# Two GNN and MoE layers on one core: the second layer's late expert tiles cut into four quarters in place of two halves

## The reference

```
x = x + gnn0(layernorm(x), adj, h0, y)
x = x + moe0(layernorm(x))        # 8 experts, hidden 512, top 2, plus a shared expert
x = x + gnn1(layernorm(x), adj, adj)
x = x + moe1(layernorm(x))        # 8 experts, hidden 256, top 2
```

```
h = gelu(xf @ w1[e] + b1[e]);  y = h @ w2[e] + b2[e];  out += cw[:, e] * y
```

## Time and profile before

| | |
|---|---|
| three timed runs, median (lowest, highest) | 1405.32 us (1403.5, 1409.83) |
| profiled execution, first to last instruction | 1406.8 us |
| PE busy | 1294.1 us, 92% |
| DVE busy | 922.4 us, 66% |
| ACT busy | 645.5 us, 46% |
| POOL busy | 426.3 us, 30% |
| scatters of y, both layers (L1882) | 144, 142.2 us, 987 ns each |
| granted clock of PE, mean | 0.977 |
| HBM read, written | 346.44 MB, 56.89 MB |

### The profile page before, as it was taken

One profiled execution on the slowest core, in us unless ns is written; L12 is line 12 of the kernel. 1 busy time (PEld: TensorE's weight loads), 2 busy tenths in 40 slices (PEclk: granted clock), 3 DMA queues, 4 the chain that ended last, 5 costly groups with the idle time before them and its releaser, 6 DMA issues.

```text
span 1406.8 us, 20911 instructions
## 1 busy us (share of the span) xinstructions
PE 1294.1 (92%) x6560; PEld 818.7 (58%) x6560; DVE 922.4 (66%) x2683; ACT 645.5 (46%) x1175; POOL 426.3 (30%) x427
## 2 busy tenths in 40 slices
PE   5899999999999999999989999999998999988950
PEld 2344445454545454554778998466666666766840
DVE  7776877777686877777542232877776777854323
ACT  3445444443434444343444554665555555543420
POOL 2102020202020202021365554302322333267772
PEclk9999999999999999999999999999999999999985
DMA  9798998889898979798559993789897988846846
GB/s 311 244 355 296 363 352 333 284 318 318 288 347 269 361 252 357 252 335 267 203 175 406 334 303 117 287 291 314 316 317 270 323 316 311 271 124 181 246 135 226
DMA packets 120974, 399.76 MB, mean 284 GB/s; under 512 B 19920, under 2 KB 51170, under 8 KB 91552
## 3 DMA queue, kind: packets, MB, share of 16 engines
q1 hardware_dynamic: 80512, 339.66, 69.1%
q10 hardware_dynamic: 28288, 34.98, 7.1%
q0 software_dynamic: 12064, 23.80, 4.6%
HBM read 346.44 MB, written 56.89 MB: 287 GB/s over the span
## 4 chain that ended last, share of the span: by engine, by line
PE 26%; DVE 11%; issue 8%; POOL 5%; DMA 2%; ACT 2%; POOLq 0%; SPq 0%; DVEq 0%; ACTq 0%
PE d L896 6%; POOL y_scratch L1882 3%; DVE adj_over_wb L398 3%; PE u L963 2%; PE agg L963 2%; PE u L880 2%; PE agg L968 1%; POOL rows_scratch L1873 1%; PE u L968 1%; PE agg L970 1%; PE agg L969 1%; PE u L970 1%; PE u L969 1%; PE u L882 1%; PE u L881 1%
## 5 line engine op out<-in xcount | busy, mean ns | idle before, releaser
L787 PE MATMUL agg<-m,xn 128*128 128x512 f32 (+1 forms) x800 | 402.8, 586 | 0.0
L1117 ACT ACTIVATE mabs<-m 128x512 f32<-128x512 f32 (+1 forms) x400 | 239.7, 617 | 309.4 <-DVE m L1635 208.6
L1635 DVE TENSOR_TENSOR m<-s,ring 128x512 f32<-128x512 f32 (+1 forms) x400 | 268.8, 675 | 149.0 <-PE s L763 128.1
L763 PE MATMUL s<-ymov,ysta 128*128 128x512 f32 (+1 forms) x400 | 263.3, 659 | 24.8 <-DVE m L1635 15.8
L1873 POOL DMA_INDIRECT rows_scratch<-xrow,idx x160 | 170.1, 1063 | 295.6 <-DVE xrow L1361 104.0
L787 PEld LDWEIGHTS agg<-m,xn 128*128 128x128 f32 x800 | 151.9, 190 | 68.5 <-issue 48.1
L1882 POOL DMA_INDIRECT y_scratch<-yo,ids x144 | 142.2, 987 | 83.5 <-issue 52.0
L763 PEld LDWEIGHTS s<-ymov,ysta 128*128 128x128 f32 x400 | 76.0, 190 | 153.7 <-issue 95.2
L398 DVE TENSOR_TENSOR adj_over_wb<-ring,adj_over_wb 128x512 fp32r<-128x512 f32 (+1 forms) x216 | 138.9, 673 | 34.5 <-ACT adj_over_wb L1220 32.1
L1220 ACT CAST adj_over_wb<-ring 128x512 fp32r<-128x512 f32 (+1 forms) x216 | 125.8, 607 | 52.4 <-PE agg L970 26.3
L1859 POOL TENSOR_TENSOR rstd<-vareps,mhalf 128x4 f32<-128x4 f32 x30 | 38.6, 1286 | 365.7 <-DVE vareps L1273 365.7
(11 more groups left out here) (278 smaller groups left out, 2270.3 us busy)
## 6 DMA issues: line engine op xcount, KB each, us to landing
ring<-in_adj_in SPq DMA_DIRECT2D x180, 1024.0 KB, 6.0
ring<-in_adj_out SPq DMA_DIRECT2D x30, 1024.0 KB, 7.8
rows_scratch<-yo ACTq DMA_DIRECT2D x81, 260.0 KB, 7.2
wb<-blob_scratch SPq DMA_DIRECT2D x24, 834.0 KB
stage<-in_adj_out SPq DMA_DIRECT2D x19, 1024.0 KB, 9.4
ring<-in_adj_in SPq DMA_DIRECT2D x20, 784.0 KB, 5.2
wb_more<-blob_scratch SPq DMA_DIRECT2D x15, 834.0 KB
xt<-rows_scratch SPq DMA_DIRECT2D x60, 130.0 KB, 4.1
```

Source lines behind the costliest of these rows:

```text
L763: pe.matmul(sbank[s % 2][:, 0:width(k)], ysta[:, s * P:(s + 1) * P], ymov[:, k % 2, 0:width(k)], start=True, stop=True).then_inc(s_made, 1)
L787: pe.matmul(abank[:, 0:n], xn[:, b, :], m[:, b % M_BUFS, 0:n], start=b == 0, stop=b == NB - 1).then_inc(S["agg_blocks"], 1)
L1117: act.activation(mabs[:, b % ABS_BUFS, 0:width(k)], m[:, b % M_BUFS, 0:width(k)], ACT.Abs).then_inc(abs_made, 1)
L1635: dve.tensor_tensor(m[:, s % M_BUFS, 0:width(k)], sbank[s % 2][:, 0:width(k)], slot_part(LOAD_AT[k, l, False][0], s % LB, width(k)), ALU.m ...
```

## The change

`PARTS` of the second layer goes from 2 to 4. A late tile then holds four quarters of 128 rows, each with its own place, expert and weights; 13 such tiles cover the worst case in place of 15, so the layer has 22 tiles. The further weights need room: `wbz_more` takes three buffers for each of two parts, and the fourth part's three buffers (`wbz_last`) lie over `stage`, `mabs` and `ymov`, which are free by then. The lists of late tiles move over `aux` and `m`, also free. The first layer's tiles and all scatters of routed rows are as before.

```
-PARTS = (2,2)
+PARTS = (2, 4)
...
-    wbz_more = over("wbz_more", [P, WB_BUFS, BLOB[1]], F32, "stage")
+    wbz_more = over("wbz_more", [P, 2, WB_BUFS, BLOB[1]], F32, "stage")
+    wbz_last = [over("wbz_last0", [P, BLOB[1]], F32, "stage", 8 * CW * 4),
+                over("wbz_last1", [P, BLOB[1]], F32, "mabs", 4 * CW * 4),
+                over("wbz_last2", [P, BLOB[1]], F32, "ymov")]
...
+    inner_quarter = sb("inner_quarter", [P, 1])
...
-    tile_e = sb("tile_e", [P, LISTED])
-    tile_row = sb("tile_row", [P, LISTED])
-    tile_end = sb("tile_end", [P, LISTED])
+    tile_e = sb("tile_e", [P, EARLY])
+    tile_row = sb("tile_row", [P, EARLY])
+    late_e, late_row, late_end = [aux[:].rearrange("p t d -> p (t d)")[:, i * P:i * P + max(LATE_PARTS)] for i in range(3)]
...
         if tile_layer(t):
-            return (wbz, wbz_more)[i][:, t % WB_BUFS, :]
+            if i == 3:
+                return wbz_last[t % WB_BUFS][:]
+            return wbz_more[:, i - 1, t % WB_BUFS, :] if i else wbz[:, t % WB_BUFS, :]
...
-            shifted = aggf[:, CW - n * E:].rearrange("p (t e) -> p t e", e=E)
+            shifted = (m[:, 1, 0:n * E] if layer else aggf[:, CW - n * E:]).rearrange("p (t e) -> p t e", e=E)
...
-            within = inner if parts == 1 else inner_half
+            within = {1: inner, 2: inner_half, 4: inner_quarter}[parts]
```

More of the change, by code:

```diff
@@ L1455, in make_table @@
             rows, at = TILE // parts, slice(EARLY, EARLY + LATE_PARTS[layer])
-            row, late, end = tile_row[:, at], tiles[:, 0:n], tile_end[:, at]
+            row, late, end, expert = late_row[:, 0:n], tiles[:, 0:n], late_end[:, 0:n], late_e[:, 0:n]
             passed = aggf[:, 0:n * E].rearrange("p (t e) -> p t e", e=E)
-            shifted = aggf[:, CW - n * E:].rearrange("p (t e) -> p t e", e=E)
+            shifted = (m[:, 1, 0:n * E] if layer else aggf[:, CW - n * E:]).rearrange("p (t e) -> p t e", e=E)
             over_limit = aggf[:, 0:E * CH * parts].rearrange("p (e c) -> p e c", e=E)
             kept = drop[:, 0:n * TB // parts].rearrange("p (t q) -> p t q", t=n)
-            within = inner if parts == 1 else inner_half
+            within = {1: inner, 2: inner_half, 4: inner_quarter}[parts]
             dve.wait_ge(posn_read, CH * (layer + 1))
@@ L1479, in make_table @@
                                    ALU.is_le))
-            dve.tensor_reduce(tile_e[:, at], passed, AX.X, ALU.add)
+            dve.tensor_reduce(expert, passed, AX.X, ALU.add)
             step(dve.tensor_tensor(shifted, passed, over_tiles(shift[:, 0, :], n), ALU.mult))
@@ L1484, in make_table @@
             dve.tensor_scalar(table[:, layer, 0, at], row, row0[:], float(LAST_ROW), ALU.add, ALU.min)
-            dve.tensor_scalar(table[:, layer, 1, at], tile_e[:, at], float(E - 1), None, ALU.min
+            dve.tensor_scalar(table[:, layer, 1, at], expert, float(E - 1), None, ALU.min
                               ).then_inc(table_made, 1)
@@ L1853, in _ @@
         pool.iota(inner_half[:], [[1, TB // 2]], base=0, channel_multiplier=TB // 2, allow_small_or_imprecise_dtypes=True)
+        pool.iota(inner_quarter[:], [[1, 1]], base=0, channel_multiplier=1, allow_small_or_imprecise_dtypes=True)
         pool.iota(tokid[:], [[P * NB, 2], [1, NB]], base=0, channel_multiplier=NB, allow_small_or_imprecise_dtypes=True
```

## The result

Five runs of the changed kernel had a median of 1443.61 us (1434.84 to 1445.47), five of the kernel before 1409.83 (1403.5 to 1411.73). The ratio is 1.0215 with a 95% interval of 1.0186 to 1.0244, so the change costs about 30 us (0.0215 of 1409.83; the two medians themselves lie 33.8 apart).

What follows compares the result with a forecast made beforehand. POOL bounds the kernel now and SP would after the change; SP's 103 steps plus 4.05, 8.1 and 4.5 us put the last scatter 33.9 us later, which added to 1405.32 gives 1439.2 us, range 1428 to 1450.

Steps and rivals of the forecast that it cites:

- The bound before: Second layer's late tiles: POOL's scatters bound the kernel, 1.30 us each, 5.2 us a tile; two tiles removed save 10.4 us.
- SP's cost per transfer: SP's late-tile loads: 1.144 us per transfer, not per byte; eight make 9.15 us a tile, above POOL's 5.2.
- Start of the late transfers unmoved by the longer table: SP's first late load: DVE's longer table adds up to 2.3 us, covered by SP's 5.5 us wait for scattered rows.
- Last weights to first product, 4.05 us: Last late tile: from the start of SP's last weight transfer to PE's first matmul, 4.05 us; lower bound 3.3.
- First product to output, 8.1 us: Last late tile: PE's first matmul to scaled output, 8.1 us at nearly the slow clock, between 6.0 and 8.9.
- Output to fourth scatter, 4.5 us: Last late tile: from its output to the start of POOL's fourth scatter, including three steps of 1.30, 4.5 us.
- the tail, 25.2: Kernel's end: from the start of the last scatter to the end of the span, 25.2 us, nothing in it edited.
- The sum: Last scatter's start: 1398.9 + 4.05 + 8.1 + 4.5 = 1415.5 against 1381.61, so +33.9 us; low case +26.7.
- DMA share near 0.8: Late tiles' transfers: 118 engine-us a tile, 7.4 us with 16 engines, fitting inside 9.15 us at a share of 0.81.
- The rivals: Four alternatives for the late tiles: POOL bound 0.03, 16 engines' pace 0.05, PE's lower clock 0.07, doubled weight traffic 0.05.
- rival 1: Late tiles: POOL stays the bound, two tiles saved, 1395; only if a transfer costs SP under 0.65 us; chance 0.03.
- rival 3: Late tiles: PE falls to the lower clock for good, 9.7 us a tile, 6.6 more, 1446; chance 0.07.

## Why the prediction was right, step by step

The mechanism was the forecast one: SP's fixed cost per transfer, times eight a tile, became the pace. Of the terms after it three were too high and the pace a little too low. The time forecast was 1439.2 and the median is 1443.61, while the kernel before rose as well, from 1405.32 when the forecast was made to 1409.83; as a ratio it was 1.0241 against 1.0215. That the medians differ by 33.8 us, as forecast to a tenth, is luck.

- **The bound before.** Right: POOL. The two saved tiles give 9 us (6 to 13 by the interval) when SP is out of the way, 7.3 against the kernel before with the same loads (1405.41 against 1412.69), predicted 10.4, and freeing SP alone gives nothing clear of noise.
- **SP's cost per transfer.** Right: 1.148 us against 1.144, at a DMA share of 0.46, 0.70 or in split halves alike. What it consists of was not: I gave the register load and its instructions all of the 0.76 us between two DMA instructions. The load with its checks is 0.56 to 0.59; the rest stays with the transfer, 0.515 with the address instruction. The bounds checks are half of the load's part.
- **Start of the late transfers unmoved by the longer table.** Right. DVE's work on the table took 8.5 us (1257.42 to 1265.92) against 6.45 (1264.52 to 1270.97), 2.1 more where I had said up to 2.3, and SP still waited for the scattered rows after it:

```profile
SPq L375 <- DMA rows_scratch<-xrow,idx: 4.4, 1, 4.4
```

- Against the 5.5 of the earlier trace rows that is only 1.1 less, since POOL's routed scatters and their landing came 0.9 us later behind the routing than before. The start itself comes 3.5 us after POOL's last routed scatter (1271.32 to 1274.86), before it was 3.1 (1277.99 to 1281.06).
- **Last weights to first product, 4.05 us.** Too high: 3.34 (1393.13 to 1396.47). The value came from a pair of transfers in a busier stretch, a DMA share of 0.87 against 0.75 here. That the lower bound, 3.3, fitted is chance: it was PE's idle time, not a time from a transfer to its landing.
- **First product to output, 8.1 us.** Too high: 7.2 (1396.47 to 1403.66). After 3.38 us of idling PE had a granted clock of 0.61 over the up products (to 1399.61) and 0.81 over the down products (to 1402.02); both are means over the two levels, 1.2 and 2.4 GHz. The tile that I took the term from had 0.58 over its products (1288.41 to 1295.30), not the 0.79 that I gave it from a window of ten microseconds. So the last tile ran faster than my nearly slow value.
- **Output to fourth scatter, 4.5 us; the tail, 25.2.** 4.6 (1403.66 to 1408.25) and 24.85 (to 1433.1).
- **The sum.** Late stretch 117.8 + 16.65 + 25.2 = 159.7 predicted, 118.3 + 15.1 + 24.85 = 158.2 measured; the difference to before +33.9 predicted, +32.5 in the late stretches of the profiles, +30.3 by the ratio of the timed runs.
- **DMA share near 0.8.** Too high: 0.69. A window of the changed kernel, in which the granted clock is 0.84 too:

```profile
1300.00:1380.00 80.00, 49.51 (x321) 47.08 (x320) 14.49 (x54) 23.90 (x79) 36.01 (x38) 0.84 0.69 204
```

- Here 71 transfers of SP took 61.2% of 16 engines in 80 us, 11.0 engine-us each (busy time added up over the engines) where I had taken 13.6 from the earlier trace rows. The x pieces have half the size now, and I had not counted that; whether it is all of the difference no run shows. The rule of the Trainium skill that I weighed there (DMA: Bandwidth & Descriptors, Issuing engines are not separate DMA queues: starting a transfer usually costs little beside it) does not describe these transfers: 1.15 us of SP against 11.0 / 16 = 0.69 us of the engines. Even against the 3.0 to 3.7 us from issue to landing of one weight transfer it is a third.
- **The rivals.** None of the four came. In rival 1 I put the point at which POOL stays the bound at 0.65 us a transfer. That was wrong: at 0.72 (5.75 us a tile on average) POOL still is, since its backlog, 20 scatters or 26 us ahead of the first late one, lets SP be slower for 13 tiles. In rival 3 the clock did fall, and it didn't matter for the pace: PE had 9 us for each tile and was busy 36 of 60.

## What to carry to other kernels

Count the transfers that one queue has to start per tile, with the register work ahead of each, and set it against the engine that bounds the tile now; here two tiles less on POOL, 10 us, were paid with 44 more starts on SP, 104 in place of 60, 50 us, of which POOL's backlog hid a part. A finer cut pays only once the starts are cheap: load all indices of a tile at once and leave out bounds checks where the table is clamped anyway. Whether starting a part of the transfers from another engine's queue would do as well, no run here tried. A slow queue is hidden for as long as the bound has a backlog, so compare totals over the stage, not paces.

## What the runs showed that I had not expected

- A bounds check of a loaded value costs SP 0.12 to 0.14 us (16 of them: 3.88 against 2.01 us between tiles; two of them: 1.10 against 0.82). Two per value, eight values a tile: about 2 us a tile.
- A load of four values costs 0.75 us (2.01 less one transfer's 0.515, for two), a load of one 0.30.
- POOL's scatters keep 1.28 us from start to start at a DMA share of 1.00 as at 0.64: 47 in 60 us in both.
